# First batch's cross stacks made by row-selecting products on TensorE instead of copies between SBUF tiles

## What is computed

```
q, k, v    = heads(x @ Wq + bq), heads(x @ Wk + bk), heads(x @ Wv + bv)
qc, kc, vc = heads(x @ Wcq + bcq), heads(c @ Wck + bck), heads(c @ Wcv + bcv)
y = softmax(causal(q kT * scale)) v + softmax(qc kcT * scale) vc
x = x + tanh(g_xattn) * (y @ Wp + bp)
x = x + tanh(g_ffn) * moe(layernorm(x))
```

## Time and profile before

| | us |
|---|---|
| median of 3 runs | 333.56 |
| lowest and highest run | 332.65 and 334.58 |
| profiled execution | 332.33 |
| its span | 330.6 |
| PE busy | 306.9 |
| DVE busy | 263.2 |
| ACT busy | 187.4 |
| POOL busy | 157.3 |

### The profile page before, as it was taken

How to read it: one execution, slowest core, us unless ns; L and a number is a source line. 1 busy time by engine, 2 the same in 40 slices (tenths; PEclk the granted TensorE clock), 3 DMA queues, 4 the chain that set the end, 5 groups by cost and what they waited for, 6 DMA issues and landing times.

```text
span 330.6 us, 8663 instructions
## 1 busy us (share of the span) xinstructions
PE 306.9 (93%) x3150; PEld 241.0 (73%) x3150; DVE 263.2 (80%) x652; ACT 187.4 (57%) x386; POOL 157.3 (48%) x189
## 2 busy tenths in 40 slices
PE   1759889999999999999999999999999999999896
PEld 1545557776787788778777878878787887787675
DVE  5799878686889899998798898878688885465873
ACT  2240555776887754857456856766566557752220
POOL 6892456473570468034803766077504450441713
PEclk9875979999999999999999999999999999999999
DMA  4363676867637695757645545275354601605012
GB/s 145 92 183 100 208 179 171 225 177 243 157 104 219 147 193 146 193 132 161 182 86 135 134 113 157 72 169 139 96 143 120 120 2 35 129 4 132 16 39 90
DMA packets 37808, 43.71 MB, mean 132 GB/s; under 512 B 4198, under 2 KB 33174, under 8 KB 35478
## 3 DMA queue, kind: packets, MB, share of 16 engines
q1 hardware_dynamic: 36542, 42.57, 51.0%
q10 hardware_dynamic: 1224, 0.59, 0.7%
HBM read 32.59 MB, written 9.18 MB: 126 GB/s over the span
## 4 chain that ended last, share of the span: by engine, by line
PE 76%; DVE 9%; DMA 8%; ACT 2%; issue 2%; SPq 1%; POOL 1%; DVEq 0%; ACTq 0%; POOLq 0%
PE bank L928 15%; PE bank L1010 14%; PE bank L885 9%; PE bank L1046 8%; PE bank L907 8%; PE bank L904 6%; PE bank L882 5%; DMA q_stack<-q_scr 4%; DVE row_max L1115 3%; DMA q_stack<-shiftT 2%; PE bank L943 2%; PE bank L982 2%; DVE k_stack L489 2%; PE bank L934 1%; PE bank L997 1%
## 5 line engine op out<-in xcount | busy, mean ns | idle before, releaser
L1115 DVE TENSOR_REDUCE row_max<-bank 128x2 f32<-128x512 f32 (+1 forms) x224 | 146.6, 685 | 28.0 <-PE bank L885 19.4
L796 ACT ACTIVATE probs<-bank 128x512 f32<-128x512 f32 x224 | 126.0, 596 | 57.2 <-PE bank L904 27.4
L1010 PE MATMUL bank<-xn2T,w_pairs_sb 128*128 128x256 f32 x256 | 66.4, 386 | 1.5 <-DVE f_gate L1195 0.9
L928 PE MATMUL bank<-probs,v_ext 128*32 128x256 f32 (+1 forms) x1024 | 55.8, 359 | 0.1
L885 PE MATMUL bank<-k_stack,q_stack 72*128 72x256 bf16 x256 | 47.1, 283 | 5.2 <-DVE row_max L1115 3.5
L1010 PEld LDWEIGHTS bank<-xn2T,w_pairs_sb 128*128 128x128 f32 x256 | 44.0, 190 | 7.8 <-DVE f_gate L1195 2.4
L708 POOL TENSOR_TENSOR f_h<-f_h,comb 128x512 f32<-128x512 f32 x31 | 38.8, 1268 | 21.9 <-DVE f_h L1203 8.2
L907 PE MATMUL bank<-q_stack,k_stack 73*128 73x256 bf16 x256 | 44.3, 275 | 0.8 <-DMA q_stack<-shiftT 0.3
L928 PEld LDWEIGHTS bank<-probs,v_ext 128*32 128x32 f32 x1024 | 29.6, 110 | 19.6 <-issue 3.6
L882 PE MATMUL bank<-k_stack,q_stack 121*128 121x128 bf16 (+1 forms) x384 | 35.6, 222 | 0.7 <-DVE row_max L1115 0.6
L885 PEld LDWEIGHTS bank<-k_stack,q_stack 72*128 72x128 bf16 x256 | 22.4, 100 | 18.2 <-DVE row_max L1115 9.8
(11 more groups left out here) (126 smaller groups left out, 369.9 us busy)
## 6 DMA issues: line engine op xcount, KB each, us to landing
k_stack<-k_scr SPq DMA_DIRECT2D x45, 192.0 KB
q_stack<-q_scr SPq DMA_DIRECT2D x15, 576.0 KB
comb<-c_scr SPq DMA_DIRECT2D x14, 512.0 KB, 6.6
q_scr<-part SPq DMA_DIRECT2D x45, 64.0 KB
k_scr<-part SPq DMA_DIRECT2D x45, 64.0 KB
v_scr<-v_out SPq DMA_DIRECT2D x8, 256.0 KB, 4.1
v_back<-v_scr SPq DMA_DIRECT2D x8, 256.0 KB, 3.7
x_in<-in_x SPq DMA_DIRECT2D x8, 128.0 KB, 3.0
```

The source lines that it names most:

```text
L796: nc.scalar.activation(probs[:, seq % NP, :], exp_bank[s % 2][:, :], ACT.Exp).then_inc(exp_done, 1)
L928: last = pe.matmul(pv_bank[32 * n:32 * n + VW, col + q0:col + T], v[:, VW // 2 * odd:VW // 2 * odd + VW], weights, start=odd == 0 and kt = ...
L1010: last = pe.matmul(bank_of[:, n * T:(n + 1) * T], w[:, e0:e0 + 128], xn2T[:, :], start=True, stop=True)
L1115: nc.vector.tensor_reduce(row_max[:, kind, h0:h0 + nh, qt], max_bank[k % 2][:, :].rearrange("p (h k) -> p h k", h=nh), AX.X, ALU.max).then ...
```

## The change

`copy_first` and the words fq and fk are gone. POOL makes two sets of columns (word cols, `make_columns`) in the part of q_stack that batch 2's cross queries will fill later: one clear of 128x3136 bf16 and four selects that set ones. PE multiplies them with the parts (word rep, `spread_rows`): for each pair of heads and each of q and k, six products of 256 columns, three parts accumulated for each of two heads, into one of the two banks of the exponentials. ACT evicts each bank as bf16 into the stack (word rep_e, `place_rows`). There are 16 such sets. A chunk of maxima now waits for the rows of its own two heads only, not for the whole stack. The part tiles of batch 0 are released by the products (`part_free`), the load of batch 2's cross queries waits for the last of them, and the first chunk of exponentials waits for all rows. All five lists are written in a new order.

```
+            def make_columns():
+                nc.gpsimd.memset(row_columns, 0.0).then_inc(columns_step, 1)
+                pool.wait_ge(columns_step, 1)
...
+                nc.gpsimd.affine_select(out=at_q, in_=at_q, compare_op=ALU.not_equal, fill=1.0, base=0,
+                                        pattern=[[-1, H], [-H, D], [0, PARTS]], channel_multiplier=1).then_inc(columns_made, 1)
...
+                for i in range(PARTS):
+                    at = at_k[:, :, i, :, 0]
+                    nc.gpsimd.affine_select(out=at, in_=at, compare_op=ALU.not_equal, fill=1.0, base=0,
+                                            pattern=[[-1, H], [-H, D]], channel_multiplier=1).then_inc(columns_made, 1)
...
+            def place_rows(m):
+                pair, qk = divmod(m, 2)
+                act.wait_ge(rows_ready, m + 1)
+                to = (q_stack, k_stack)[qk][0:STACK, 0, CROSS, 2 * pair:2 * pair + 2, :]
+                nc.scalar.activation(to, exp_bank[qk][0:STACK, :].rearrange("p (h x) -> p h x", h=2), ACT.Copy).then_inc(rows_placed, 1)
...
+            def spread_rows(m):
+                pair, qk = divmod(m, 2)
+                if m == 0:
+                    pe.wait_ge(columns_made, 1 + PARTS)
+                ge(pe, rows_placed, m - 1)
+                for e in range(2):
+                    h = 2 * pair + e
+                    for n in range(PARTS):
+                        pe.wait_ge(split[CROSS], n + 1)
+                        if qk == 0:
+                            cols = q_columns[:, h, STACK - BLOCK - n * BLOCK:2 * STACK - BLOCK - n * BLOCK]
+                        else:
+                            cols = k_columns[:, h, PARTS - 1 - n:PARTS - 1 - n + STACK]
+                        last = pe.matmul(exp_bank[qk][0:STACK, e * T:(e + 1) * T], cols, part[:, CROSS, n, qk * T:(qk + 1) * T],
+                                         start=e == 0 and n == 0, stop=e == 1 and n == PARTS - 1)
+                last.then_inc(rows_ready, 1)
...
-                if k in (0, CROSS_C1):
+                if b == 0 and kind == CROSS:
+                    pe.wait_ge(rows_placed, h0 + nh)
+                elif k in (0, CROSS_C1):
                     stack_here(pe, b, kind)
...
     'pool': '''
-        masks:0 rstd1:0 masks:0:1 rstd1:1 xn1:1 rstd1:2 rows:0 xn1:2 vclear:0 sp1:1:1 vclear:0:1 rstd1:3 sp3:1:1 xn1:3
+        masks:0 rstd1:0 masks:0:1 rstd1:1 cols:0 xn1:1 rstd1:2 xn1:2 vclear:0 vclear:0:1 rows:0 sp1:1:1 sp3:1:1 rstd1:3
```

More of the change, by code:

```diff
@@ L93 @@
     'pe': '''
[L94 to L103, removed]
@@ L119 @@
[L119 to L128, removed]
@@ new lines @@
+        xnT:0 proj:0 proj:0:1 vproj:0 rep:0 rep:0:1 xnT:1 rep:0:2 rep:0:3 max:0 rep:0:4 rep:0:5 max:0:1 rep:0:6 rep:0:7
+        max:0:2 rep:0:8 rep:0:9 proj:1 rep:0:10 rep:0:11 proj:1:1 rep:0:12 rep:0:13 max:0:3 max:0:4 rep:0:14 rep:0:15
+        max:0:5 max:0:6 vproj:1 max:0:7 xnT:2 max:0:8 max:0:9 shift:0 proj:2:1 vproj:2 max:0:10 max:0:11 exp:0 exp:0:1
+        max:0:12 max:0:13 exp:0:2 max:0:14 proj:2 max:0:15 exp:0:3 max:0:16 exp:0:4 shift:0:2 max:0:17 max:0:18 exp:0:5
+        max:0:19 max:0:20 xnT:3 exp:0:6 exp:0:7 max:0:21 max:0:22 proj:3 max:0:23 max:0:24 exp:0:8 exp:0:9 max:0:25 pv:0
@@ new lines @@
+        max:0:26 max:0:27 exp:0:10 exp:0:11 max:1 exp:0:12 max:1:1 exp:0:13 shift:0:1 max:1:2 exp:0:14 max:1:3 vproj:3
+        max:1:4 max:1:5 proj:3:1 max:1:6 exp:0:15 max:1:7 exp:0:16 max:1:8 pv:0:1 max:1:9 max:1:10 exp:0:17 exp:0:18
+        xnT:4 max:1:11 max:1:12 exp:0:19 exp:0:20 max:1:13 vproj:4 exp:0:21 max:1:14 max:1:15 exp:0:22 proj:4 exp:0:23
+        max:1:16 max:1:17 proj:4:1 exp:0:24 shift:1 max:1:18 max:1:19 pv:0:2 max:1:20 exp:0:25 exp:0:26 max:1:21
+        max:1:22 exp:0:27 y:0 exp:1 max:1:23 max:1:24 exp:1:1 pv:0:3 exp:1:2 max:1:25 xnT:5 exp:1:3 max:1:26 exp:1:4
@@ new lines @@
+        exp:3:21 up:1:1 max:4:17 max:4:18 exp:3:22 exp:3:23 pv:3:2 exp:3:24 max:4:19 exp:3:25 shift:4 up:1:2 exp:3:26
+        exp:3:27 max:4:20 max:4:21 ga:1:3 max:4:22 pv:3:3 exp:4 max:4:23 max:4:24 xn2T:2 up:1:3 exp:4:1 exp:4:2 max:4:25
+        max:4:26 logits:2 down:1 exp:4:3 down:1:1 exp:4:4 max:4:27 exp:4:5 xnT:6 max:5 down:1:2 down:1:3 exp:4:6 exp:4:7
+        shift:4:1 max:5:1 max:5:2 down:1:4 down:1:5 y:3 exp:4:8 exp:4:9 max:5:3 down:1:6 down:1:7 max:5:4 max:5:5 pv:4
+        exp:4:10 exp:4:11 ga:2 exp:4:12 max:5:6 combT:2 up:2 exp:4:13 exp:4:14 proj:6 max:5:7 max:5:8 exp:4:15 ga:2:1
@@ new lines @@
+        max:6:6 up:3 exp:5:9 exp:5:10 xnT:7 pv:5 exp:5:11 proj:7 down:2:3 max:6:7 exp:5:12 exp:5:13 max:6:8 down:2:4
+        combT:3 max:6:9 exp:5:14 max:6:10 down:2:5 down:2:6 max:6:11 down:2:7 max:6:12 exp:5:15 y:4:1 exp:5:16 ga:3
+        max:6:13 proj:7:1 max:6:14 max:6:15 pv:5:1 max:6:16 ga:3:1 max:6:17 exp:5:17 shift:6 exp:5:18 max:6:18 up:3:1
+        max:6:19 max:6:20 yT:4 exp:5:19 ga:3:2 exp:5:20 exp:5:21 max:6:21 max:6:22 up:3:2 exp:5:22 wp:4 max:6:23
+        exp:5:23 exp:5:24 pv:5:2 exp:5:25 y:5 max:6:24 exp:5:26 max:6:25 exp:5:27 ga:3:3 exp:6 exp:6:1 up:3:3 exp:6:2
@@ L412, in stores_of_part, with part_free @@
         def stores_of_part(b, kind):
[L414 removed]
+            return 32 * (b + (kind == SELF))
+        def part_free(eng, b, kind, n):
+            if b == 1 and kind == CROSS:
+                eng.wait_ge(rows_ready, SPREADS)
+            elif b > 0:
+                eng.wait_ge(part_out[kind][n], stores_of_part(b - 1, kind))
         def stack_here(eng, b, kind):
             if b == 0 and kind == CROSS:
[L418 to L419 removed]
+                eng.wait_ge(rows_placed, SPREADS)
             elif b >= 0:
@@ L712, in _ @@
                     make_masks(n)
+                elif what == "cols":
+                    make_columns()
                 elif what == "rows":
@@ L820, in _ @@
                     gate_values()
+                elif what == "rep_e":
+                    place_rows(n)
                 elif what == "xnT_e":
```

276 lines of the change are left out of this document (136 added, 140 removed).

## The result

The changed kernel takes 340.37 us (median of 4 runs, 339.12 to 341.88), the kernel before 334.07 (4 runs, 332.65 to 335.32): ratio 1.019, 95% interval 1.013 to 1.026. It is slower by 6.3 us; the forecast was 336.8, in a range to 341.0. The profiled execution of after took 341.88, with a span of 340.2 us, 9.6 more than that of before; it lies 1.5 over its median, as that of before lay 1.2 under its own.

The account below looks back on a forecast made before the run. DVE was taken to bound the kernel ahead of 50 us, PE behind. Eighth maximum 7.8 us later, partly given back, left +3.2 us at the 50.05 us place: 336.8 us from the median 333.56, range 331.8 to 341.0.

Parts of the forecast that it names:

- the rival in which TensorE stays at the low level: Row products and projections keep running at the low clock level: about +8 us, 341.5 us; chance 0.15.
- Step 1: POOL makes the selecting columns behind batch 1's rstd: 6.1 us, so they stand at 16.9 us.
- Steps 2 to 4: Row products, ScalarE's evictions, then DVE's four remaining mask copies: eighth maximum taken at 37.0 us, 7.8 us later.
- Step 5: Eighth to last maximum of batch 0: delay partly given back, place reached at 53.2 us against 50.05.
- its transfer 4.40: The second shift's transfer, on the chain from sixteenth to last maximum, taken as 4.40 us from the trace of before.
- the value products 1.86 at the high level: Value products behind the second shift and two chunks of exponentials, taken as 1.86 us at the high clock level.
- the place of the forecast: Where batch 0's last maximum product, first value products and batch 3's cross projection are all done: 53.2 us against 50.05.
- step 4: DVE still owes four mask copies and statistics behind the second maximum: third maximum at 31.6 us, eighth at 37.0.
- PE unbroken behind that: Sign: behind batch 0's last maximum near 53.7 us PE runs unbroken; idle time behind 55 us within 1 us of before.
- The early columns: Rival: columns at 14.0 us, PE stays at the high level, eighth maximum at 31.0, 330.9 us; chance 0.20.
- "no change" rival: The products fit into PE's idle time in the first 48 us: 333.6 to 334 us; chance 0.20.

Follow-up runs that it names:

- f2: Old order with products, but columns made first on POOL, mask copies spread between first maxima, second-batch projections later, self loads ahead of stores: 337.44 us, ratio 1.008.
- e4: The changed kernel with four mask copies moved from behind the second maximum to behind batch 0's last and batch 1's eleventh: 345.88 us, ratio 1.034.
- e3: The changed kernel with only the first of three bf16 parts in the row products, 32 of 96 products remaining: 341.98 us, ratio 1.019.
- f3: f2 with zeros under the columns set by VectorE, selects behind POOL's masks, one mask copy of each kind ahead of the splits: 333.45 us, ratio 0.999.
- e1: The changed kernel with batch 0's second shift row (4 KB) issued ahead of the 576 KB load of cross queries: 342.22 us, ratio 1.018.
- f5: The kernel before with 18 transposes of the identity at TensorE's start and nothing else: 333.74 us, ratio 0.998.
- f6: f3 with VectorE's clear behind its constants, second-batch projections between last row products and their maxima, second-batch values evicted earlier: 334.55 us, ratio 1.002.
- f8: f3 with only the first of three parts in the row products, 64 of 96 products left out: 333.31 us, ratio 0.999.
- f4: f3 with 18 transposes of the identity at TensorE's start, which nothing reads: 333.48 us, ratio 0.998.

## Why the prediction was right, and where it fell short

The side and the range were right, and the steps up to the sixteenth maximum held. That the range holds the time is in part luck: 340.37 lies 0.6 us under its end, and that end was drawn for the rival in which TensorE stays at the low level, which did not happen. The delay was forecast at 3.2 us and came out at 6.3.

**Step 1 held**: the first row product was forecast at 16.9 and came at 17.33. The prices behind it were off in both directions. POOL's timeline in after:

```profile
9.90 2.72 POOL L651 MEMSET q_stack<- 128x3136 bf16 x1
12.77 2.85 POOL L654 TENSOR_SCALAR_AFFINE_SELECT q_stack<-q_stack 128x384 bf16<-128x384 bf16 x1
15.57 1.71 POOL L659 TENSOR_SCALAR_AFFINE_SELECT q_stack<-q_stack 128x128 bf16<-128x128 bf16 x3
```

The clear goes by elements, as taken (2.72; 2.8 forecast). The selects took 4.6 in place of 3.1, and POOL came to them 0.8 earlier, so that the place fits to 0.4 us is in part luck. The q select lay beside the mask copy of q_stack (12.73 us; the prediction had that of k_stack there); in f2, without one, it took 1.85. That 1.0 us is the term that the Trainium skill, SBUF — State Buffer, "Who interferes with whom", would have added (1.2 forecast by it): the trace agrees with the rule, and my value by the rows did not have it.

**Steps 2 to 4 held.** Level up by 22 (22.5 forecast), first maximum taken at 23.6 (23.65), second at 25.1 (25.3), eighth at 37.2 (37.0). The four mask copies took 6.6 us and not 4.9, the third maximum was taken at 33.1 and not 31.6, and TensorE was behind by then anyway, as e4 shows.

**Step 5 failed, in two terms.** The sixteenth maximum came at 44.5 (44.4). Then "its transfer 4.40" took 8.32, and "the value products 1.86 at the high level" took 3.57. That is 3.9 and 1.7 us, together 5.6 of the 6.0 by which the place of the forecast came late (59.2 for 53.2). There is a wrong reading too: in before the shift, two maximum chunks and the first value products stand ahead of proj:3, which ends at 50.6 and not at 50.05, so step 5 should have given +2.6. With the two terms it would have been +8.2 us of span, and +9.6 was measured.

Both terms I could have doubted. The transfer came from a row of before in which the shift followed the 576 KB load by 2.06 us. By my own step 4 the load and the shift both come later, and nothing kept their distance. Over the traces kept here the shift took longer the closer it was issued behind that load: 8.32 us at 1.43 (after), 6.95 at 1.58 (e3), 4.40 at 2.06 (before), at most 3.1 at 3.45 (f3). No run varied this distance alone, so that it is the reason is not shown. For the value products, before's own first ones took 2.6 us, and I took the later 1.86; in the pause for the shift the granted clock fell to 0.64 and then read 0.50 beside them. e1 shows that mending the shift is not enough: with the shift ahead of the load, the key loads are what TensorE waits for.

**"PE unbroken behind that" held**: 8.0 us idle in the last 275.7 (7.7 in before).

**The rivals.** The early columns decided as named: f3's first row product comes ahead of 15 us, the level stays up, the eighth maximum is taken at 29.5 (31.0 in that rival). But the time is then 333.45, not 330.9, so it ends as the "no change" rival. For before, the prediction had VectorE's mask copies as the bound ahead of the first maximum; f5 bears that out. In f3 VectorE and TensorE are both full: from 14 to 29.4 TensorE has no wait over 0.4 us, and VectorE waits 1.4 us in all. f6 and f8 fit this: an earlier start does not move the eighth maximum, and with fewer products VectorE's own work still lasts until 28. Which of f3's moves carries how much of the 7 us was not taken apart further; f2 to f3 is 4 of them.

## What to carry to other kernels

Having an operand earlier is worth nothing while another engine sets the pace at that place; look for who starts late through the new way of making it. When a step comes later, do not carry over the duration of a transfer behind it from the old trace: list what shares its queue at the new time, look how close behind a large load it is issued, and see what stands behind its consumer on an in-order engine. If one edit only moves a wait elsewhere, as e1, e3 and e4 did, plan the whole stretch anew.

## What the runs showed of the hardware

- A 4 KB transfer in the queue behind a 576 KB load took 8.32 us when issued 1.43 us behind it, 4.40 at 2.06 us (before) and at most 3.1 at 3.45 us (f3); in after the DMA engines were 97% busy in its last but one microsecond.
- Beside POOL's clear of 3136 bf16 a VectorE step of 0.93 us took 2.77 (f2). The same clear took 2.72 us on POOL and 1.36 on VectorE (f3), where it ran as 1568 32-bit elements:

```profile
2.38 1.36 DVE L1126 MEMSET q_stack<- 128x1568 uint32 x1 [0.39 <-issue]
```

- Behind eighteen fp32 transposes at the very start a product of the first projections took 0.59 us in f5 (1.06 in before), as at the high level, but 1.06 in f4.
- The granted clock reads 1.00 at the start of after, and the trace's first record of the clock comes at 11.3 us. Two products of the same kind took 1.03 us at 10.45 and 0.62 at 11.30, both under a reading of 1.00. So a reading from ahead of the first record says nothing about the level; the duration of a product does.
